# A fused Flamingo block on one core: the probabilities-times-V product as one step in the middle of the next group, in place of two half steps

## The reference

```python
scores = einsum('bqhd,bkhd->bhqk', q, k) * scale
attn = softmax(scores, axis=-1)
out = einsum('bhqk,bkhd->bqhd', attn, v)
```

## Time and profile before

| | |
|---|---|
| median of three runs | 1231.31 us |
| the profiled execution | 1225.18 us, span 1223.4 us |
| mean granted clock of TensorE | 0.936 of full speed |
| PE / PEld busy | 1064.0 us (87%) / 655.8 us |
| DVE / ACT / POOL busy | 778.9 / 618.0 / 389.2 us |
| product, L1633 | 3072 instructions |
| layers by time from the start (us) | att0 to 386, att1 to 624, att2 to 901, att3 to 1087, experts to 1223 |

### The profile page before, as it was taken

How to read it: one execution, slowest core, us unless ns; L and a number is a source line. 1 busy time by engine, 2 the same in 40 slices (tenths; PEclk the granted TensorE clock), 3 DMA queues, 4 the chain that set the end, 5 groups by cost and what they waited for, 6 DMA issues and landing times. The chain is left out here.

```text
span 1223.4 us, 25244 instructions
## 1 busy us (share of the span) xinstructions
PE 1064.0 (87%) x8548; PEld 655.8 (54%) x8548; DVE 778.9 (64%) x1887; ACT 618.0 (51%) x1331; POOL 389.2 (32%) x1034
## 2 busy tenths in 40 slices
PE   3999997899988678688899988998989889899998
PEld 1355553577554566344455544444556567655665
DVE  3788888334877213476788868678774776645543
ACT  1377765455664333355567765654644344543221
POOL 3433333421444311554533334313242434200000
PEclk9999999899896789788899999898998999999999
DMA  7555545454345343555666543523333455200000
GB/s 195 152 168 179 169 148 155 145 163 123 109 125 168 102 135 118 149 162 160 193 192 179 155 144 120 169 92 118 110 121 118 128 155 169 88 27 28 26 20 16
DMA packets 173877, 158.76 MB, mean 130 GB/s; under 512 B 13011, under 2 KB 147539, under 8 KB 173395
## 3 DMA queue, kind: packets, MB, share of 16 engines
q1 hardware_dynamic: 169558, 142.03, 39.3%
q0 software_dynamic: 4192, 15.12, 4.0%
HBM read 91.56 MB, written 67.63 MB: 130 GB/s over the span
## 5 line engine op out<-in xcount | busy, mean ns | idle before, releaser
L1087 ACT ACTIVATE prob<-ps 128x512 f32<-128x512 f32 (+1 forms) x768 | 399.0, 579 | 181.4 <-PE ps L1617 137.5
L1267 DVE TENSOR_REDUCE nmax<-ps 128x1 f32<-128x512 f32 x512 | 329.1, 684 | 97.2 <-PE ps L1582 95.2
L1617 PE MATMUL ps<-Qst,Kst 75*128 75x256 bf16 x1408 | 243.4, 284 | 11.3 <-DMA Qst<-mrow 8.2
L1582 PE MATMUL ps<-Kst,Qst 72*128 72x512 bf16 x512 | 198.9, 405 | 23.6 <-DVE nmax L1267 19.5
L1633 PE MATMUL av_ps<-prob,Vx 128*32 128x256 f32 (+1 forms) x3072 | 218.3, 401 | 0.0
L1617 PEld LDWEIGHTS ps<-Qst,Kst 75*128 75x128 bf16 x1408 | 136.7, 101 | 79.9 <-DMA Qst<-mrow 12.9
L1009 POOL TENSOR_TENSOR mparts<-nmax,zeros 128x8 bf16<-128x8 f32 x128 | 25.9, 203 | 325.5 <-issue 316.9
L1633 PEld LDWEIGHTS av_ps<-prob,Vx 128*32 128x32 f32 x3072 | 92.7, 114 | 67.3 <-issue 37.2
L1276 DVE TENSOR_REDUCE nmax<-ps 128x2 f32<-128x512 f32 x128 | 85.8, 687 | 58.8 <-PE ps L1596 57.4
L1582 PEld LDWEIGHTS ps<-Kst,Qst 72*128 72x128 bf16 x512 | 50.8, 100 | 105.5 <-DVE nmax L1267 48.3
L1091 ACT ACTIVATE OT<-av_ps 128x256 f32<-128x256 f32 x128 | 49.3, 385 | 105.3 <-PE av_ps L1633 104.6
(11 more groups left out here) (190 smaller groups left out, 1677.4 us busy)
## 6 DMA issues: line engine op xcount, KB each, us to landing
k_parts<-kp SPq DMA_DIRECT2D x48, 384.0 KB
q_parts<-qp SPq DMA_DIRECT2D x96, 192.0 KB, 2.6
Qst<-q_parts SPq DMA_DIRECT2D x128, 144.0 KB
Kst<-k_parts SPq DMA_DIRECT2D x64, 288.0 KB
k_parts<-kp SPq DMA_DIRECT2D x48, 192.0 KB
Kst<-k_parts SPq DMA_DIRECT2D x64, 144.0 KB
ctxT<-in_ctxT SPq DMA_DIRECT2D x16, 256.0 KB, 5.0
xs_rows<-in_blank SPq DMA_DIRECT2D x22, 128.0 KB, 4.0
```

What stands on the lines that cost most here:

```text
L1087: act.activation(prob[:, RING_AT[st] % RING, half * 512:half * 512 + w], bank(x)[:, 0:w], ACT.Exp).then_inc(drained(x), 1)
L1267: ve.tensor_reduce(nmax[:, g, u, h % GH:h % GH + 1], bank(st), AX.X, ALU.max, negate=True).then_inc(drained(st), 1)
L1582: last = pe.matmul(bank(st), Qst[0:ROWS, par, s, u * P:u * P + P], Ks[0:ROWS, par, s, :], start=True, stop=True)
L1617: last = pe.matmul(o, Ks[0:KROWS, par, h, t * P:t * P + P], Qst[0:KROWS, par, h, :], start=True, stop=not a.rope)
```

## The change

`avs` goes. With 512 keys, a product step now covers all four key tiles of a group (32 matmul instructions) and stands in the third slot of the next group, `s % gs == gs // 2`: slots 2, 6, 10 and 14 of a batch. The wait for the group's last exponential and for the bank stands ahead of it, as before ahead of the first half. For 256 keys `gs // 2` is 1, which is where the product stood; of these layers only the last product of batch 15, which falls into batch 16, moves from slot 3 to slot 2. The last products of batches 7 and 23 fall into layers of 256 keys: their halves in slots 0 and 1 become one step in slot 1.

```diff
@@ class Att
-        self.avs = self.kt // 2
@@ body
         if s >= a.gs:
-            product = [("AV", n, (s // a.gs - 1, x)) for x in range(a.avs) if (x + 1) * a.gs // a.avs - 1 == s % a.gs]
+            product = [("AV", n, s // a.gs - 1)] if s % a.gs == a.gs // 2 else []
         elif n > lo:
-            p = att(n - 1)
-            product = [("AV", n - 1, (NG - 1, x)) for x in range(p.avs) if (x + 1) * a.gs // p.avs - 1 == s]
+            product = [("AV", n - 1, NG - 1)] if s == a.gs // 2 else []
         if product:
             units.insert(max(1, len(units) - 1), product)
@@ moe1_steps
-    out = [("loadres", n, None)] + [("AV", n, (NG - 1, p)) for p in range(att(n).avs)]
+    out = [("loadres", n, None)] + [("AV", n, NG - 1)]
@@ order of the bank av_ps
-GROUP = count(("AV", "f.down"), lambda st: st[0] != "AV" or st[2][1] == att(st[1]).avs - 1)
+GROUP = count(("AV", "f.down"))
@@ ScalarE
-                elif kind == "AV" and st in GROUP:
+                elif kind == "AV":
                     act.wait_ge(av_filled, GROUP[st] + 1)
-                    act.activation(OT[:, n % 2, arg[0], :], av_ps[:, 0:SQ], ACT.Copy).then_inc(av_drained, 1)
+                    act.activation(OT[:, n % 2, arg, :], av_ps[:, 0:SQ], ACT.Copy).then_inc(av_drained, 1)
@@ TensorE
                 elif kind == "AV":
-                    g, t0 = arg
-                    if t0 == 0:
-                        wait_drained(pe, (("E", n, (g + 1) * a.gs - 1), 1))
-                        if group(n, g):
-                            pe.wait_ge(av_drained, group(n, g))
-                    for t in range(t0 * a.kt // a.avs, (t0 + 1) * a.kt // a.avs):
+                    g = arg
+                    wait_drained(pe, (("E", n, (g + 1) * a.gs - 1), 1))
+                    if group(n, g):
+                        pe.wait_ge(av_drained, group(n, g))
+                    for t in range(a.kt):
                         for hh in range(GH):
...
-                    if t0 == a.avs - 1:
-                        last.then_inc(av_filled, 1)
+                    last.then_inc(av_filled, 1)
```

More of the change, by code:

```diff
@@ L473 @@
 BANK = banks()
-GROUP = count(("AV", "f.down"), lambda st: st[0] != "AV" or st[2][1] == att(st[1]).avs - 1)
+GROUP = count(("AV", "f.down"))
 def group(n, g):
-    return GROUP[("AV", n, (g, att(n).avs - 1))]
+    return GROUP[("AV", n, g)]
 def heads_half(n, h):
```

## The result

The change made the kernel slower: **1266.5 us** (1260.9 to 1274.5, 6 runs) against 1230.4 us (1216.1 to 1239.1, 6 runs), a ratio of **1.0332 [1.0294, 1.0371]**. The profiled execution took 1266.38 us, with a span of 1264.6 us and a mean granted clock of 0.912, against 1225.18, 1223.4 and 0.936 before. The forecast was 1233 us, and 1260 the end of its range: it was wrong. The two medians are 36 us apart, the two profiled executions 41 (1264.6 - 1223.4), and all of these 41 us lie in the two layers with 512 keys. att2 is measured from the load of batch 15's residual rows to that of batch 23's, and went from 277.1 to 299.4 us (+22.3). att0 is measured from 56 us after the start to the load of batch 7's rows, and went from 301.7 to 320.7 (+19.0).

What follows compares the result with a forecast made beforehand. PE was taken to set the pace, with DVE close behind. Terms of -3 - 9 + 7 + 7 = +2 us on the profiled 1225.2, with the runs' median 6 us higher, gave 1233 us; range 1212 to 1260, own range 1218 to 1250.

Steps and rivals of the forecast that it cites:

- PE's work per group: On PE in the 512-key layers: 2.71 us per group after against 2.70 before, so nothing over 64 groups.
- Rival 2: Faster: second half runs at its loads' pace, maxT's visit falls into a wait; 30 us go, 1203; chance 0.08.
- The term for separated groups: Where something stands between maxT and the product, 3.18 us becomes 2.71; 6 groups of 64, -3 us.
- Stalls at the single bank: At PE's single small-step bank: ctx's wait gone, -9 us; waits for maxT's bank, +7; xT in att0, +7.
- the +5 of the sum: The single small-step bank's terms taken together: -9, +7 and +7 us.
- Rival 3: Stalls at the single bank reach their upper bound: +28 in place of +14, 1247; chance within the forecast's 0.75.
- DVE's supply, costed at nothing: Three S banks hold 2.05 us against 2.3 needed per group; shortfall 0.3, below DVE's 0.75 idle time: 0 us.
- Rival 1: S banks aren't full when PE turns to the product, DVE starves: 33 us slower, 1266; chance 0.17.

Runs made afterwards that it cites:

- the filler: The kernel after plus a thrown-away half product in each att0 batch (slot 11) and att2 batch (slot 9); 1245.5 us, ratio 1.016 to the kernel before.
- the last run: From the kernel before: in att2 the product whole behind maxT and resid moved to slot 9 under it, att0 unchanged; 1234.5 us, ratio 1.013.

## Why the prediction was wrong

**PE's work per group: right.** From the product's first load to the next full load it is 1.86 us, and maxT is followed by a full load after 0.21, to the hundredth as forecast:

```profile
678.29 0.09 PEld L1659 LDWEIGHTS ps<-identb,mparts 128*12 128x12 bf16 x2 [0.34 <-ACTq L1110]
678.50 0.10 PEld L1579 LDWEIGHTS ps<-Kst,Qst 72*128 72x128 bf16 x1
...
679.75 0.42 PEld L1568 LDWEIGHTS ps<-ident,OT 128*128 128x128 f32 x4 [0.51 <-ACT mrow L1116]
...
680.34 1.45 PEld L1629 LDWEIGHTS av_ps<-prob,Vx 128*32 128x32 f32 x32 [0.17 <-issue]
682.20 0.10 PEld L1579 LDWEIGHTS ps<-Kst,Qst 72*128 72x128 bf16 x1 [0.41 <-issue]
```

Rival 2, with its faster product, is refuted by the same rows. The term for separated groups has the right sign: batch 5, with two such groups (0.9 us in the sum), went from 76.4 to 74.4 us.

**Stalls at the single bank: right in kind, a few us too low.** In the plain att2 batch the wait for `att_o` ahead of ctx's second part is gone (0.57 us). In its place ctx's first part waits 0.51 us for ACT's copy, in the rows above, and the small step of another slot 0.24. Over att0 and att2 together PE's waits for ACT's copy of maxT went from nothing to 12.0 us, where 14 were taken, and its waits for `att_o` from 10.0 to 6.1, 3.8 less, where 9 were taken: the old wait stood in 10 of the 16 batches. That is +8 us of waits for the +5 of the sum. xT itself waits 0.25 us in one plain batch of att0 (0.8 was taken in each, and 0.8 x 8 is 6.4, not 7). Rival 3, with +28, isn't what happened.

**DVE's supply, costed at nothing: this step failed**, in its two halves. It asked only what happens *behind* the product, and there it found a mean shortfall of 0.3 us. At full clock the change costs about 1.3 us per plain batch: 1.25 in the pair with the half-wide maximum, 30.78 - 1.7 - 27.78 = 1.3 in the kernel after without its clock stretch, 1.39 in the batch with the filler. As an estimate that is 16 x 1.3 = 21 us, where 0 had been taken. But it never asked what PE does at the place that the half product *leaves*. Its argument that the three banks "should fill" between products treats full banks as pure cover for DVE. Full banks also stop PE. The earlier trace rows listed DVE's own work in ctx's and v's slots, and not the residual and the norm's sums, 0.42 + 0.49 + 0.25 us in a row, which stand in the trace of before just where a half product was. The wait of 0.7 us in the earlier trace rows was that place: what was left of the pause with a half product in it.

The second half of the failure is **the clock**. No term of the sum had it, although the span before already had a granted clock of 0.936, and the plain batches 1.00. In the plain att2 batch, a gap longer by 1.0 us cost about 2.7, since the fall behind it brought 1.7 us more. Of the 41 us in the two layers, the low clock goes with 34 (56 - 22 of full clock lost). That is an upper bound: 21 and 34 are more than 41, so part of either lies under other waits.

**Rival 1** had the right time (1266) and the right symptom, DVE idle for well over 4 us. Its mechanism, too few units in the banks when PE turns to the product, isn't the main one: with the reduction at half its length three quarters of the loss stayed, att0 lost 11 us with no product joined, and the filler gave 21 us back with every product whole. It had neither the pause nor the clock, so that its number was hit is chance. A smaller part for it isn't excluded. The run with four banks can't say, as E lost one for it, and the last run, with no pause in slot 9, still lost 2.5 us in a plain batch.

**What stays open.** In att0 the filler gave back only 2 of 19 us, its own eight half products (some 9 us of PE's work) counted, and moving the norm work 7. The empty fourth slots account for 11 of the 19, by the run with halves in the second and third slot. How these divide over the places, and where the other 8 come from, isn't shown. Why two halves around a unit are 11 us slower than one product isn't settled between the third visit to narrow weights and the clock, which was low there as well. That the pause brings on the fall of the clock is well borne out in att2: over the plain batches 16 to 18 of all kernels, 10 of 10 pauses of 1.62 or 1.63 us had the half clock behind them, 0 of 13 pauses of 1.06 to 1.08. (In two of the ten the fall began in the last 0.5 us of the pause, in the others within 1 us after it.) In batches 1 to 3 of att0 a fall began within 2 us of the end of 11 of 17 pauses of 1.63 to 1.83 us, and falls without a long pause occur in both. So a pause makes a fall likely; what decides each case isn't shown.

## What to carry to other kernels

Before a step is moved out of a place, ask what the other engine does at that place: a step that looks like load on the busiest engine may be the filler of a wait, and taking it away opens a gap rather than saving time. List the other engine's side work (norms, divisions, biases) by slot, and put the steps that need nothing from it exactly there. Where TensorE runs dense at full clock, price a new gap by itself and by the stretch of half clock that may follow it: here 1.0 us and 1.7 us.

## What the runs showed of the hardware

In plain batches that otherwise run at full clock, a pause of 1.6 us on TensorE was followed by a granted clock of half (1.2 of 2.4 GHz) in 10 of 10 cases in att2, mostly within 1 us, and in att0 in 11 of 17 (pauses up to 1.83 us). Such a stretch lasted 3.4 or 6.8 us, in one case 13.7, and lost half of that in full clock. With the pause at 0.66 us (before), 0.73 (four S banks) or 1.06 (filler), batch 17 kept 1.00 throughout. Two waits of 0.84 and 0.50 us close together had a fall behind them as well. Work that is thrown away made this kernel 21 us faster in one slot, and in another the same work gave nothing back (9 us slower, at the edge of the noise).
